# A fused attention and mixture-of-LoRA block: sums divided by rows after a way through DRAM, x loaded by columns

## The reference

```
x = x + attention(layernorm(x)) # 16 heads of 16, causal, then o_proj; layernorms have no weights
z = layernorm(x)
base  = z @ W.T + b
gates = softmax(top2(z @ gate_w.T + gate_b)) # 8 experts
delta = sum over the 2 chosen experts of gates * (z @ lora_A[e].T @ lora_B[e].T) # rank 16
out = x + base + delta
```

## Time and profile before

| | |
|---|---|
| median of 3 runs | 394.41 us (393.88 to 394.71) |
| profiled execution | 393.18 us, of which the span from first to last instruction is 391.4 |
| TensorE (PE) busy | 354.2 us, 90% |
| ScalarE (ACT) busy | 279.5 us, 71% |
| VectorE (DVE) busy | 209.7 us, 54% |
| GpSimd (POOL) busy | 47.8 us, 12% |
| mean granted TensorE clock | 0.975 |
| first exponential | 22.11 us from the span's start |
| last sums copied | 365.3 to 366.0 us |

### The profile page before, as it was taken

One profiled execution on the slowest core, in us unless ns is written; L12 is line 12 of the kernel. 1 busy time (PEld: TensorE's weight loads), 2 busy tenths in 40 slices (PEclk: granted clock), 3 DMA queues, 4 the chain that ended last, 5 costly groups with the idle time before them and its releaser, 6 DMA issues.

```text
span 391.4 us, 6977 instructions
## 1 busy us (share of the span) xinstructions
PE 354.2 (90%) x2558; PEld 138.0 (35%) x2558; DVE 209.7 (54%) x711; ACT 279.5 (71%) x317; POOL 47.8 (12%) x75
## 2 busy tenths in 40 slices
PE   8967978899998999999999999998999899799874
PEld 3545524354333444423323233232322323222542
DVE  4555558455755654555447464546346543600785
ACT  2544438677887877888788887888878688799311
POOL 5011000000011100011121111211112111100040
PEclk9997969999999999999999999999999999999997
DMA  6479444222450022271000000000000000000001
GB/s 202 139 224 315 116 131 141 55 55 54 124 148 13 2 54 75 62 214 44 13 2 13 3 13 16 3 13 2 13 16 0 16 0 15 13 2 3 0 3 55
DMA packets 29380, 23.31 MB, mean 60 GB/s; under 512 B 15392, under 2 KB 25888, under 8 KB 29344
## 3 DMA queue, kind: packets, MB, share of 16 engines
q1 hardware_dynamic: 29344, 22.84, 19.8%
HBM read 12.35 MB, written 10.49 MB: 58 GB/s over the span
## 4 chain that ended last, share of the span: by engine, by line
PE 63%; DVE 20%; ACT 7%; issue 6%; POOL 2%; DMA 1%; DVEq 0%; ACTq 0%
PE acc L713 23%; PE scores L696 12%; PE aux L596 7%; ACT probs L814 6%; PE aux L651 5%; PE aux L637 3%; DVE probs L1010 2%; PE aux L662 2%; PE aux L602 2%; PE aux L623 1%; DVE ffn L1055 1%; POOL exp_gap L1216 1%; PE aux L644 1%; DVE gates L1083 1%; DVE parts L954 1%
## 5 line engine op out<-in xcount | busy, mean ns | idle before, releaser
L814 ACT ACTIVATE probs<-scores 128x1024 f32<-128x1024 f32 x272 | 260.2, 1032 | 69.1 <-PE scores L696 59.1
L713 PE MATMUL acc<-probs,v_aug 128*32 128x512 f32 (+3 forms) x1280 | 145.4, 545 | 1.3 <-ACT probs L814 0.9
L696 PE MATMUL scores<-q_stack,k_stack 64*128 64x512 f16 (+3 forms) x640 | 86.5, 352 | 3.7 <-ACT probs L814 2.0
L696 PEld LDWEIGHTS scores<-q_stack,k_stack 64*128 64x128 f16 x640 | 21.1, 94 | 103.6 <-ACT probs L814 80.3
L1010 DVE TENSOR_TENSOR probs<-probs,mask_sb 128x512 f32<-128x512 f32 (+1 forms) x80 | 44.2, 577 | 22.5 <-ACT probs L814 22.0
L713 PEld LDWEIGHTS acc<-probs,v_aug 128*32 128x32 f32 x1280 | 30.8, 110 | 49.8 <-issue 29.7
L596 PE MATMUL aux<-xT,wqkv_sb 128*128 128x128 f32 x192 | 26.3, 294 | 1.0 <-DVE xT L941 1.0
L596 PEld LDWEIGHTS aux<-xT,wqkv_sb 128*128 128x128 f32 x192 | 24.0, 203 | 5.4 <-issue 3.1
L952 DVE CAST parts<-qk 128x512 f16<-128x512 f32 x12 | 5.1, 427 | 36.5 <-ACT qk L806 36.5
L1207 POOL TENSOR_TENSOR rstd<-ve,minus_half 128x1 f32<-128x1 f32 x12 | 7.3, 608 | 101.6 <-DVE ve L932 101.6
L1211 POOL TENSOR_TENSOR rstd<-ve,minus_half 128x1 f32<-128x1 f32 x12 | 6.6, 549 | 103.8 <-DVE ve L1040 103.8
(11 more groups left out here) (146 smaller groups left out, 323.0 us busy)
## 6 DMA issues: line engine op xcount, KB each, us to landing
q_stack<-q_dram SPq DMA_DIRECT2D x32, 128.0 KB, 2.8
k_stack<-k_dram SPq DMA_DIRECT2D x32, 128.0 KB, 2.8
qk_dram<-qk SPq DMA_DIRECT2D x12, 256.0 KB, 2.5
x_sb<-x SPq DMA_DIRECT2D x3, 512.0 KB, 6.4
q_dram<-parts SPq DMA_DIRECT2D x12, 128.0 KB, 2.0
k_dram<-parts SPq DMA_DIRECT2D x48, 32.0 KB, 1.9
out<-result SPq DMA_DIRECT2D x12, 128.0 KB, 1.7
qk_dram<-probs SPq DMA_DIRECT2D x4, 256.0 KB, 3.3
```

The source lines that it names most:

```text
L696: m = pe.matmul(scores[u % BANKS][:, j, col:col + n], k_stack[row:row + STACK, kb // TPC, 2 * i + p, kb % TPC * P:(kb % TPC + 1) * P], q_s ...
L713: m = pe.matmul(acc[32 * hp:32 * hp + 32, lo:CHUNK], v_aug[:, kb, QUAD * i + hp, :], probs[:, u % PROBS, hp % 2, col:col + CHUNK - lo], st ...
L814: act.activation(probs[:, u % PROBS], scores[u % BANKS][:], ACT.Exp, scale=EXP_SCALE).then_inc(exp_done, 1)
```

## The change

- **Sums.** Behind the second and fourth quad of a chunk SP stores two blocks of sums to DRAM (`store_sums`) and, a step later, loads them back with four DMAs (`load_sums`) so that numerators of all eight heads fill 128 partitions, feature by head, in one array and the denominators, one copy for each feature, another. `divide` is now a 128x128 reciprocal and product per tile and half, at `DIVIDE_AT`: from four steps behind the sums, one tile a step. `o` takes the quotients as they are; the rows of o's weights are reordered on the host. `turn_sums` and `turn_back` are gone from the loop.
- **x.** The host also gives x by columns (`x_t`); SP loads a chunk of it into `xT`. `measure_x` still works on rows, for four tiles, in steps from `MEASURE_FROM`. POOL takes the power of all four, stores means and scales to DRAM (elements of 4 bytes) and loads them back to all partitions as two rows of 512, both DMAs on its own queue. `normalise_x` subtracts and multiplies with these rows, 512 columns a pass, for each half. `turn_x` is gone. For chunk 1 both passes stand at step 1 of VectorE.
- **Pieces.** `project_qk` is one block of 512 columns (four a chunk), `project_v` as before. For chunk 1 they are placed from step 2 on, two a step; for chunks 2 and 3 from two steps behind `NORMALISE_FROM` on, so steps 17 to 26 and 43 to 52 with the norms. The two buffers of `qk32` and `parts` are now one for q and one for k. The stacks' first halves are loaded behind the second Q/K piece, the others behind the fourth.
- **Tail.** The first half of the last chunk is divided in the loop. `residual` puts x (by a product with the identity) and o's first half into the tiles' banks at step 137, ahead of its groups. The second half is turned as before, at half the width; ScalarE copies y out (`keep_y`), where VectorE added x.
- **First chunk.** Its measuring of chunk 1 goes between the splits, ahead of the squares; the turn of chunk 1's first tile is gone from it.

```diff
+DIVIDE_LAG = 4
...
+            for t in range(TPC):
+                at.setdefault(s + DIVIDE_LAG + t, []).append((c, m, t))
...
+FIRST_PIECE = 2
+MEASURE_FROM = {c: FIRST_STEP[c - 1] - 3 for c in range(2, NCHUNK)}
+NORMALISE_FROM = {c: MEASURE_FROM[c] + TPC + 4 for c in range(2, NCHUNK)}
+POST_PIECES = ("o", "turn_y", "ffn", "turn_gated", "lora")
+POST_GAP = {"o": 2, "turn_y": 1, "ffn": 2, "turn_gated": 1, "lora": 1}
...
+            qk = [("project_qk", len(FIRST) * c + n) for n in range(len(FIRST))]
+            v = [("project_v", TPC * (c + 1) + t) for t in range(TPC)]
+            pre = [p for both in zip(qk, v) for p in both] if c == 0 else qk + v
...
+                if pre and s >= (FIRST_PIECE if c == 0 else NORMALISE_FROM[c + 1] + 2):
...
+                if len(flying) < 2 and post_next < TILES - TPC and s > DIVIDED_STEP[post_next // TPC]:
...
+            def load_xT(c):
+                sp.wait_ge(v_psum, TPC * (c - 1))
+                sp.dma_start(xT[:], x_t[c]).then_inc(xT_in[c], 16)
...
+            def store_sums(c, m):
+                sp.wait_ge(acc_read, NQUAD * c + 2 * m + 2)
+                sp.dma_start(sums_dram[c, m], sums[:, 2 * m:2 * m + 2, :]).then_inc(sums_out[m], 16)
+
+            def load_sums(c, m):
+                sp.wait_ge(sums_out[m], 16 * (c + 1))
+                if c >= 2:
+                    sp.wait_ge(o_psum, TPC * (c - 1))
+                rows = sums_dram[c, m].rearrange("(h n d) q t -> n q d h t", h=QUAD, n=2)
+                for n in range(2):
+                    for q in range(2):
+                        sp.dma_start(attn[q * P // 2:(q + 1) * P // 2, c % 2, m, n], rows[n, q]).then_inc(sums_in[m], 16)
...
+            def project_qk(n):
+                c, (kq, b) = n // len(FIRST) + 1, FIRST[n % len(FIRST)]
+                pe.wait_ge(xT_ready, KH * c)
+                col = column_of(kq, b)
                 for k in range(KH):
+                    m = pe.matmul(aux[:], wqkv_sb[:, k, col:col + P], xT[:, k, :],
+                                  start=(k == 0), stop=(k == KH - 1))
                 m.then_inc(qk_psum, 1)
...
+            def residual(n, w):
+                pe.wait_ge(exp_done, tail_units[n % TPC] + 1)
+                pe.matmul(w.bank[:, 0:D], ident_sb[:], x_sb[:, n, :], start=True, stop=False)
+                pe.wait_ge(divided, divided_upto(NCHUNK - 1, 0, n % TPC))
+                pe.matmul(w.bank[:, 0:D], attn_of(n, 0), wo_sb[:, 0, :], start=False, stop=False)
...
+            def normalise_x(c, k):
+                n = KH * (c - 1) + k + 1
+                dve.wait_ge(xT_in[c], 16)
+                dve.wait_ge(rows_in, 16 * c)
+                x_rows = xT[:, k, :]
+                dve.tensor_tensor(x_rows, x_rows, rows[c % 2][:, 0, :], ALU.subtract).then_inc(centred, 1)
+                dve.wait_ge(centred, n)
+                dve.tensor_tensor(x_rows, x_rows, rows[c % 2][:, 1, :], ALU.mult).then_inc(xT_ready, 1)
...
+                if c:
+                    dve.wait_ge(sums_out[i // 2], 16 * c)
+                dve.tensor_copy(sums[:, i, :], acc[:]).then_inc(acc_read, 1)
+
+            def divide(c, m, t):
+                n = divided_upto(c, m, t)
+                num, den = (attn[:, c % 2, m, n, t * P:(t + 1) * P] for n in range(2))
+                if t == 0:
+                    dve.wait_ge(sums_in[m], 64 * (c + 1))
+                dve.reciprocal(den, den).then_inc(inverse_ready, 1)
+                dve.wait_ge(inverse_ready, n)
+                dve.tensor_tensor(num, num, den, ALU.mult).then_inc(divided, 1)
...
+            def rstd_x(c):
+                pool.wait_ge(stats1, STATS1 * c)
+                if c > 1:
+                    pool.wait_ge(rows_out, 16 * (c - 1))
+                pool.tensor_tensor(rows1[:, 1, :], ve1[:].rearrange("p t o -> p (t o)"), minus_half[:],
+                                   ALU.pow).then_inc(rstd1_ready, 1)
+                pool.wait_ge(means_ready, c)
+                pool.wait_ge(rstd1_ready, c)
+                pool.dma_start(rows_dram[c].rearrange("n (t p) -> p n t", p=P), rows1[:],
+                               allow_slow_non_contiguous=True).then_inc(rows_out, 16)
+                pool.wait_ge(rows_out, 16 * c)
+                if c > 1:
+                    pool.wait_ge(scores_ready, FIRST_UNIT[c - 1])
+                else:
+                    pool.wait_ge(squared, len(FIRST))
+                    for m in range(KH):
+                        pool.wait_ge(first_q_out[m], 16)
+                        pool.wait_ge(first_k_out[m], 16 * 2)
+                pool.dma_start(rows[c % 2], rows_dram[c].partition_broadcast(P)).then_inc(rows_in, 16)
```

More of the change, by code:

```diff
@@ L722, in step @@
                 piece(s, 0)
+                if s == STEPS - 1:
+                    for t in range(TPC):
+                        run_piece("residual", TILES - TPC + t)
                 for n in GROUPS_AT.get(s, ()):
@@ L1135, in step @@
                         keep_sums(n)
+                for c, m, t in DIVIDE_AT.get(s, ()):
+                    divide(c, m, t)
                 if (s, 1) in PIECE_AT:
```

419 lines of the change are left out of this document (230 added, 189 removed).

## The result

The changed kernel takes 431.71 us (median of 4 runs, 430.86 to 434.6) where the kernel before takes 394.14 (median of 4 runs beside it, 393.67 to 394.71): 1.0965 times as long, 95% interval 1.0911 to 1.102. Predicted were 391.1, range 383.5 to 400. The profiled execution took 431.34 us, its span is 429.5.

A forecast was written before the change was run, and what follows sets the result against it. Each loop step was taken as bound by the larger of two ScalarE exponentials (1.81 us) and TensorE's sum. Terms -10.2, -3.1, +9, -1, +2 gave -3.3 us, from 394.4 to 391.1 us, range 383.5 to 400.

The forecast's parts named there:

- Term 4: Chunk 0, with means and scales going through DRAM as rows: 1 us less, from 4 less to 5 more.
- The rival: Rows of means and scales come late in chunk 0, columns ready at 38, giving 398 us; chance 0.14.
- Term 3: Divides and other added VectorE work in the loop, holding up TensorE: 9 us more, bounds 3 and 16.
- The second rival: The divide is the bound: a reciprocal of 1.2 us on VectorE, giving 395.8 us; chance 0.16.
- the larger-of sums: Loop time with each step the larger of 1.81 us and TensorE's sum: 65.5, 100.4, 116.6 for chunks 1 to 3.
- Term 2: TensorE's waits at the gated ranks' turn, mostly behind o's projection now: 5.6 becomes 2.5, 3.1 us less, bounds 0 and 5.
- the rule: A loop step takes the larger of 1.81 us and TensorE's sum; pieces up to 0.28 us are free.
- Term 1: TensorE's loop work, turns gone and Q/K in 512-column pieces: 10.2 us less, bounds 5.5 to 12.
- the fourth rival: The turns were free, as ScalarE held the light steps: 5.5 us saved on TensorE, 395.8 us; chance 0.10.
- Term 5: Tail, residuals ahead of step 137's sums against fewer turns and no add: 2 us more, 2 less to 4 more.

The follow-up runs named there:

- e11: Changed kernel with columns of chunks 2 and 3 normalised 5 steps later and the rows' load issued 6 steps after their store: 437.44 us.
- e2: Changed kernel storing means and scales in 32-byte runs, which leaves x wrong; only the loop is read, ending 20.7 us earlier than the changed kernel's.
- e12: Changed kernel with means and scales turned on VectorE by 32x32 blocks before a store in 128-byte runs: 414.09 us.
- e3: Changed kernel with the loop's 28 reciprocals cut to one column each, other columns multiplied by their denominators: 426.4 us.
- e8: e6 with the reciprocals cut to one column each, sums multiplied by their denominators: 401.42 us.
- e6: e1 with the divides eight steps behind the sums instead of four: 410.89 us.
- e1: Changed kernel with x turned tile by tile on TensorE as before, sums still through DRAM: 417.81 us, 1.0613 times the kernel before.
- e13: e12 with the gated turn's copy ahead of the next tile's normalising and the tail's residual behind the last sums: 404.4 us, ratio 1.0272.
- e14: e13 with the divides six steps behind the sums instead of four: 400.85 us, ratio 1.0176.
- e9: e6 with the tail's residual late and the gated turn's copy ahead of the next tile's normalising on VectorE: 400.64 us, 1.0142 times the kernel before.
- e10: Changed kernel with the gated turn's copy ahead of the next tile's normalising on VectorE: 426.55 us.
- e5: Changed kernel with the divides eight steps behind the sums instead of four: 439.18 us.

## Why the prediction was wrong

**Term 4, the rows' way (-1 said, +10.7 in chunk 0 and more behind it): the step that failed.** The store of 4-byte elements was priced from the smallest stores, 1.9 us, up to 6.4; it takes 10. The rival named the cause and kept it to chunk 0. It acts in chunks 1 and 2 as well: on the columns, and on the gates' exponential behind POOL's wait; a third way, through the sums' store on another queue, is hidden behind the first two and shows in e11. e2 and e12 measure the whole at 20.7 and 17.6 us, near half of the 37.6. What of this is chunk 0's half clock cannot be told apart; with the fast store TensorE still idles 6.2 us there in e2 and its first Q/K takes 3.75. Nor is the way of the rows free with the fast store: in e12 VectorE still waits 4.8 us for them in step 15.

**Term 3, the divides (+9 said).** The reciprocal was right, 944 ns against 0.87; an estimate of 1.2 from the Trainium skill ("VectorE: DVE Perf Modes", "First, the fixed hardware budget") would have been too high. The second rival is out with it: from 1.1 us it was to decide. The size of the term failed: with the slow store gone, chunks 1 and 2 lie 9.6 and 15.8 us over the larger-of sums (e12: 75.1 and 116.2 against 65.5 and 100.4), where 6.2 and 2.8, and 2.5 for term 2 in all chunks, were added. The prediction named the places, steps 15 and 16 and 28 to 31, and gave chunk 1 6.2 us for them. Of its two reasons one is not what the trace shows: in the changed kernel the divides of step 15 on wait for no load, as VectorE is held there by the rows first, and of its waits for loads only 0.8 us lie ahead of chunk 3. The other, VectorE's load, was priced too low: step 30 lasts 6.95 us and step 33 5.91, with no wait for a DMA in either, step 30 still 6.84 in e12. Behind TensorE's idle times there the granted clock is 0.50, 1.2 GHz (138.5 to 141.9, 148.7 to 152.1). In TensorE's timeline of the changed kernel, the FFN product that the earlier trace rows has at 1.58 us:
```profile
138.46 2.95 PE L735 MATMUL aux<-wffn_sb,yT 128*128 128x392 f32 x4 [2.23 <-DVE yT L1154]
```
What the parts cost was measured in kernels with other neighbours, so they do not sum: the reciprocals' own work 3.3 and 0.7 us in chunks 1 and 2 (e3), or 4.7 and 4.6 with x on its old way (e8 against e6); the divides' place, with their wait for the loads, up to 11.7 in chunk 1 there (e1 against e6); the late turn of the rows 3.5 in chunk 1 (e13 against e14). How the rest of the 9.6 and 15.8 divides was not shown; 1.0 of each is Q/K's, below.

**Term 2, the gated turn's waits (-3.1 said).** The distance was computed on TensorE alone. With o in the step ahead of the turn, VectorE has o's tile to normalise between the turn and its copy, and POOL's scale to wait for. The wait moved to lora, in chunk 2 above all, where gated turn and lora wait 15.1 of their 18.6 us. In chunk 3 the term held: 2.5 us over the rule were said, and 119.1 is 2.5 over 116.6. The order alone is worth 4.0 us in e9 and 5.2 in e10.

**Term 1, TensorE's work (-10.2 said): right for the turns, wrong for Q/K.** Chunk 3 is 119.1 (118.8 said), a step without a piece still 1.81 us, so the fourth rival is out. But Q/K in pieces of 512 columns takes 1.98 us, no less than sixteen of 128 columns did, and the pieces in steps 44 to 46 follow at 3.45 us (3.25 said). The price of 1.72 came from first-chunk records less an estimated drain. That is 2 us of the term. A timeline row of the changed kernel's TensorE:
```profile
54.58 1.98 PE L668 MATMUL aux<-xT,wqkv_sb 128*128 128x512 f32 x4
```

**Term 5, the tail (+2 said, +1.8 seen): right in number, in part by luck.** The reason holds: in every run with the residual ahead, the last sums' copy starts 4.7 us behind the last exponential, with the residual late 1.6, so it costs 3.1 (3.8 said). The saving behind it, 1.8 said, is 1.3 in the changed kernel: 24.8 us from that copy to the end, 26.1 before. With the same tail it takes 24.5 to 24.8 us in e5, e6 and e8 too, but 26.2 to 26.5 in e1, e3, e10, e11 and e12, where there is no saving and the tail is 3.3 to 3.6 over that before. What differs is the granted clock from 5 to 15 us behind the copy, 1.00 in the four and 0.83 in the five; the changed kernel, then e12:
```profile
409.79:419.79 10.00, 7.21 (x27) 3.97 (x27) 8.05 (x51) 2.36 (x9) 4.75 (x8) 1.00 0.01 2
```
```profile
390.84:400.84 10.00, 8.45 (x26) 4.68 (x27) 6.62 (x39) 2.15 (x8) 4.74 (x8) 0.83 0.00 0
```
Why it falls in some and not in others is open. It also means that some 1.7 us of every difference between a kernel of the one group and one of the other come with the tail's clock.

Why a range of 383.5 to 400 missed 431.7: each term's bounds were set by itself, and the terms act together. A late row holds a divide and the masks, a late divide holds the turn of the rows (e12), and behind the long idle times of TensorE its records here run at 1.2 GHz.

**Open:** how the 11 and 12 us that e13 and e14 keep over the rule in chunk 2 divide among its steps was not tried. Nor was a divide of packed sums (one value for each head and token, not sixteen), which by e8 against e6 could save up to 9 us, an estimate.

## What to carry to other kernels

Turn small results until a store has long runs: 4 KB in 4-byte elements took 10 us to land, delayed a 512 KB store on another queue from 2.6 to 9.9 us, and cost 18 us in all; 0.2 us on VectorE removed that. When pieces change places on one engine, write out the order on every engine that serves them, since a copy behind another tile's work becomes the next piece's wait. An operation that waits for a DMA stops all that stands behind it on its engine, so its slack is counted to the landing of the last load, and a mean load of half says nothing of it. Whether such a wait costs anything depends on what stands behind it: two of 7 us in chunk 3 cost nothing, one of 1.2 us ahead of the turned rows (e13) was part of the 3.5 us that e14 gains in chunk 1.

## What the runs showed of the hardware

- A store of 1,024 elements of 4 bytes lands 10.0 and 10.3 us after its issue, the same bytes in 32-byte runs 1.4, turned and in 128-byte runs (16 KB) 2.6 and 3.2 (POOL's waits for the rows of chunks 2 and 3 in the changed kernel, e2 and e12).
- While it is under way, a store issued on another engine's queue lands late as well: 9.9 and 9.2 us in the changed kernel and 9.8 in e11, instead of 2.6.
- POOL takes 0.54 to 1.1 us to issue a DMA, and no other row of POOL falls into that time (changed kernel, e2, e12).
- A reciprocal of 128x128 takes 944 ns on VectorE (mean of 28 in the changed kernel), where a product of the same shape takes from 290 ns, 327 in the mean.
- With the same tail code the granted clock from 5 to 15 us behind the last sums' copy is 1.00 in four kernels and 0.83 in five, and the tail some 1.7 us longer in the five.
